# Stores of V, a reciprocal and the loads of new keys and values, moved between queues and steps of a transformer-layer kernel

## The chip, the cores and the metric

The kernel runs as one program on one core of a Trainium2 chip. The metric is the device time of that core in microseconds; the kernel before took 1255.03 us (median of three runs, 1254.48 to 1257.87).

A core has five engines with instruction queues of their own: TensorE (PE, matmuls), VectorE (DVE), ScalarE (ACT), GpSimd (POOL) and SyncE (SP), which only issues transfers here. They work on SBUF and PSUM and wait for each other by semaphores. A transfer is issued by an engine's queue (SPq, ACTq) and carried by 16 DMA engines.

## The reference

The layer is attention over paged keys and values, a long convolution of its output, and a feed-forward part with adapters, each added to its input. What the change touches is attention:

```python
q = rope(rmsnorm(x @ Wq.T)); k = rope(rmsnorm(x @ Wk.T)); v = x @ Wv.T
kc = k_cache[block_table].reshape(bsz, L, HK, D)     # 16 pages of 32 tokens
vc = v_cache[block_table].reshape(bsz, L, HK, D)
k_all = jnp.concatenate([kc, k], axis=1)             # 512 + 32 tokens
v_all = jnp.concatenate([vc, v], axis=1)
scores = jnp.einsum('bqhd,bkhd->bhqk', q, k_all) * SCALE
probs = jax.nn.softmax(jnp.where(valid, scores, -1e30), axis=-1)
o = jnp.einsum('bhqk,bkhd->bqhd', probs, v_all) @ Wo.T
```

There are 32 batches of 32 tokens, 32 query heads and 8 key/value heads (HK) of 128 (D), all in float32.

## The kernel before

The work is done in two halves of 16 batches (HB). A half projects V, K and Q of its 512 tokens, goes through attention batch by batch, and then through the output product, the convolution and the feed-forward part. Each engine has a program written out by hand; the order within an engine is the order of its code, and semaphores tie the engines together. Loops over batches go two batches at a time, one for each of two sets of key and value buffers (`par`).

**The new keys and values** of the half are stored to DRAM (`k_new`, `v_new`) and loaded again per batch in the layout that attention wants. V has two column halves of four tiles each. The first (`store_v(0, m)`) is computed at the start and stored by SyncE (L454 to L457). The second is computed last, when attention has already begun: ScalarE copies each tile out of PSUM (L707), waits for its own copy and issues the store (L712). The staging buffer has two places, so tiles 2 and 3 wait for the store of the tile two before.

**SyncE in attention** (`load_kv`) issues for each batch 16 key pages of 128 KB (L470), the batch's new keys (L475), then, when `v_free` allows it, its new values (L480) and 16 value pages (L485). Batch 0 and 1 are loaded piecemeal ahead of the loop; the new values of both wait for all stores of V (`vn_out`).

**A step of attention** is one key/value head `g` of one batch; four steps are a quad, since GU = 4 and the last head of a quad is computed without the split into high and low parts. For step s:

- ScalarE makes the high part of the keys for step s + 2 (L815) in three of four steps, takes the exponential of step s with its row sum (L856), and does in certain steps the copies of q (L807, L808), of the output (L841), the spread of the new probabilities (L834) and the mask (L820, L821).
- GpSimd makes the low part of the keys (L630) in three of four steps, and then scales the probabilities of step s - 2 by the reciprocal of their row sum (L616 for the new tokens, L618 for the 512 cached ones).
- TensorE computes the scores in six matmuls (L1084 to L1095; it waits for the low part of the keys ahead of L1090) or two (L1072, L1074), turns the scaled probabilities of step s - 3 (L1107) and multiplies those of step s - 4 with the values (L1139). Once per quad it adds the new values (L1149, `values_new`).
- VectorE adds the mask and takes the row minimum (L1636), copies the turned probabilities of step s - 3 out of PSUM (L1642), waits for the exponential of step s and takes the reciprocal of its row sum (L1649). In steps 1 and 5 of a batch it then makes the low part of q for the next quad (L1595, `lower_q`).

The probabilities go through a ring of four places, `prob0` and three in `ring`.

Of the kernel before, what the change touches and what calls it, by code (L numbers as in the profile page):

```python
# [13 lines left out]
ds = bass.ds  # L14
# [91 lines left out]
def build(nc, xT_d, w_d, amat_d, bmT_d, kpages_d, vpages_d, lA_d, lB_d, rows_d, vcT_d, bp_d, dls_d,  # L106
# [6 lines left out]
    with ExitStack() as ctx:  # L113
# [290 lines left out]
        def _(sp):  # L404
# [46 lines left out]
            load_w(0, 3)  # L451

            with sp.Fori(0, HALVES) as h:
                for k, m in enumerate((2, 3, 0, 1)):  # L454
                    sp.wait_ge(v_read, h * (2 * TILES) + k + 1)
                    sp.dma_start(vn_d[ds(h * HB + 4 * m, 4), :, 0:D].rearrange("b (t a) d -> (b t) a d", a=GU),
                                 v_stage(0, m).rearrange("p (a d) -> p a d", a=GU)).then_inc(vn_out[m % 2], 16)  # L457
                with sp.Fori(0, 2) as i:
                    for n in range(4, 8):
                        load_w(h, n, i)  # L460
# [28 lines left out]
                def load_kv(b, par):  # L489
                    pages = page_registers(b)  # L490
                    sp.wait_ge(k_free, h * HB + b - 1)
                    load_key_pages(par, pages, 0, NPP)
                    load_new_keys(b, par)
                    sp.wait_ge(v_free, h * (HB - 1) + b - 1)
                    load_new_values(b, par, v_in[par])
                    for j in range(NPP):
                        load_value_page(par, j, pages[j])

# [15 lines left out]
                for j in range(NPP):  # L514
                    if j % 4 == 0:

                        sp.wait_ge(turned, NQK * (h + 1) - 6 + 2 * (j // 4))
                        sp.sem_inc(sp_past, 1)
                    load_value_page(0, j, pages[j])
                sp.wait_ge(proj_ready, PROJ * (h + 1))  # L520
                sp.sem_inc(sp_past, 1)
                pages = page_registers(1)
                load_key_pages(1, pages, 8, NPP)
                load_new_keys(1, 1)
                for n in range(2):
                    sp.wait_ge(vn_out[n], 8 * KU * (h + 1))
                load_new_values(0, 0, first_vnew_in)
# [138 lines left out]
        def _(act):  # L666
# [18 lines left out]
            with act.Fori(0, HALVES) as h:  # L685
# [10 lines left out]
                def store_v(col, m):  # L696

                    unit = m if col == 0 else TILES + NQK + m
                    act.wait_ge(proj_ready, h * PROJ + unit + 1)
                    if col == 0:  # L700
                        pass
                    elif m < 2:

                        act.wait_ge(kn_out[m % 2], 8 * KU * (h + 1))
                    else:
                        act.wait_ge(vn_out[m % 2], h * (8 * KU) + 48)
                    nc.scalar.activation(v_stage(col, m), bank(m if col == 1 and m < 2 else 4 + m), ACT.Copy)\  # L707
                        .then_inc(v_read, 1)
                    if col == 0:
                        return  # L710
                    act.wait_ge(v_read, h * (2 * TILES) + TILES + m + 1)
                    act.dma_start(vn_d[ds(h * HB + 4 * m, 4), :, D:2 * D]  # L712
                                  .rearrange("b (t a) d -> (b t) a d", a=GU),
                                  v_stage(1, m).rearrange("p (a d) -> p a d", a=GU))\
                        .then_inc(vn_out[m % 2], 16)

                def squares(n, i=0):

# [118 lines left out]
                def keep_o(b, u):  # L837
# [3 lines left out]
                    nc.scalar.activation(qo[:, ds(b * (HQ * SEQ) + u * GU * D, GU * D)], bank(6 + u), ACT.Copy)\  # L841
                        .then_inc(ot_read, 1)

                def step(b, par, g, first, last=False):
                    s = h * STEPS + b * HK + g
                    if (g + 2) % GU < NS and not (last and g + 2 >= HK):
# [18 lines left out]
                        keep_o(b - 1, g // GU)  # L865
                    if g == 3 and not last:
                        mask_of(b + 1, 1 - par)

                act.wait_ge(turn_read, h * NQK + NQK - LAG)
                upper_q(0, 0)  # L870
# [469 lines left out]
        def _(dve):  # L1340
# [181 lines left out]
            with dve.Fori(0, HALVES) as h:  # L1522
# [100 lines left out]
                def step(b, par, g, first):  # L1623
                    s = h * STEPS + b * HK + g
                    if g < HK:
# [5 lines left out]
                        if first and g == 1:  # L1631
# [3 lines left out]
                        at = 1024 * (g % 2) + 512 - SPLIT * PSIZE  # L1635
                        V.tensor_tensor_reduce(prob(g % PRING)[:, 0:LK], PS[:, at:at + LK], mask[:, par, :],  # L1636
                                               rq[:, par, g:g + 1], 3.0e38, ALU.add, ALU.min, smin[:, g:g + 1]).then_inc(masked, 1)
                    if not (first and g < 3):
                        dve.wait_ge(pt_ready, s - 2)
                        if not (first and g < 5):  # L1640
                            dve.wait_ge(pv_done, s - 4)
                        V.tensor_copy(probT[:, (g - 3) % 2, :], bank(4)).then_inc(pt_main, 1)  # L1642
                    if first and g == 1:
                        dve.wait_ge(exp_done, s)
                        V.reciprocal(rinv[:, 0:1], rsum[:, 0:1]).then_inc(rinv_ready, 1)
                    if g < HK and not (first and g == 0):

                        dve.wait_ge(exp_done, s + 1)
                        V.reciprocal(rinv[:, g:g + 1], rsum[:, g:g + 1]).then_inc(rinv_ready, 1)  # L1649
                        if g % GU == 1:  # L1650
                            nb, u = (b, 1) if g == 1 else ((b + 1) % HB, 0)
                            dve.wait_ge(qhi_ready, h * (QUADS + 1) + b * UNITS + g // GU + 2)
                            dve.sem_inc(dve_past, 1)
                            lower_q(u, ds(nb * (HQ * SEQ) + u * GU * D, NS * D))

                for g in range(HK):
                    step(0, 0, g, True)
# [196 lines left out]
```

## Time and profile before

| | |
|---|---|
| time, median of three runs | 1255.03 us |
| time of the profiled execution | 1256.73 us |
| its span | 1254.8 us |
| TensorE busy | 1228.1 us (98%) |
| VectorE, ScalarE, GpSimd busy | 808.2, 788.1, 749.5 us |
| granted TensorE clock | full |
| read from and written to HBM | 203.33 and 10.49 MB, 170 GB/s over the span |
| attention, first half | about 160 to 476 us |
| attention, second half | about 785 to 1100 us |

Busy time is the sum of an engine's instructions. Ends of matmuls are modelled, so a busy TensorE is not TensorE at its peak. A time in a timeline is counted from the start of the span. Line numbers in the profile are those of the kernel before; behind the change lines have other numbers.

### The profile page before, as it was taken

How to read it: one execution, taken by the hardware profiler on the slowest of the kernel's cores; microseconds unless marked ns; L12 is line 12 of the kernel's file. 1: busy time of each engine (PE TensorE's matmuls, PEld its weight loads, DVE VectorE, ACT ScalarE, POOL GpSimd, SP SyncE). 2: the span in 40 equal slices, each digit the busy share in tenths (PEclk: the TensorE clock that was granted, in tenths of full speed). 3: DMA queues.
4: the chain of work that ended last, by engine and by line, in shares of the span. 5: the costliest groups of instructions: out<-in, count | busy, mean ns of one | idle time of the engine just before them, and what ended most of it. 6: DMA issues, size and time to landing. Idle time of an engine off the chain costs nothing.

```text
span 1254.8 us, 28770 instructions
## 1 busy us (share of the span) xinstructions
PE 1228.1 (98%) x7378; PEld 1031.9 (82%) x7378; DVE 808.2 (64%) x1736; ACT 788.1 (63%) x2259; POOL 749.5 (60%) x884
## 2 busy tenths in 40 slices
PE   7999999999999999999999999999999999999998
PEld 6788888899999997865777888888999999888756
DVE  6976666667666778951459667666766676655422
ACT  5666677778777774432346666777777777744320
POOL 4343467888888875433233443788888888844320
PEclk9999999999999999999999999999999999999999
DMA  6524288998999955306135252998899999534300
GB/s 206 194 92 149 95 232 220 230 232 233 236 236 237 229 159 177 142 8 194 68 105 184 84 172 91 243 220 227 224 234 240 231 238 239 121 116 153 89 30 34
DMA packets 147978, 214.82 MB, mean 171 GB/s; under 512 B 24949, under 2 KB 119479, under 8 KB 142136
## 3 DMA queue, kind: packets, MB, share of 16 engines
q1 hardware_dynamic: 134792, 206.96, 60.2%
q10 hardware_dynamic: 13104, 6.94, 1.9%
q8 instruction: 30, 0.49, 0.2%
q14 instruction: 52, 0.43, 0.1%
HBM read 203.33 MB, written 10.49 MB: 170 GB/s over the span
## 4 chain that ended last, share of the span: by engine, by line
PE 74%; SPq 15%; issue 5%; DVE 3%; ACT 1%; DMA 1%; ACTq 0%; DVEq 0%
PE PS L1139 12%; PE PS L1107 6%; SPq L485 6%; SPq L470 6%; PE PS L1206 5%; PE PS L1197 5%; PE PS L1001 5%; PE PS L1203 5%; PE PS L1005 5%; PE PS L999 5%; PE PS L1149 3%; PE PS L1248 2%; PE PS L985 2%; PE PS L1072 2%; PE PS L1237 1%
## 5 line engine op out<-in xcount | busy, mean ns | idle before, releaser
L630 POOL TENSOR_TENSOR kv_parts<-kv,k_hi 128x544 fp32r<-128x544 f32 x192 | 258.4, 1346 | 59.9 <-ACT k_hi L815 59.7
L1139 PE MATMUL PS<-probT,kv 128*128 128x128 f32 x2048 | 270.3, 275 | 0.0
L590 POOL TENSOR_TENSOR ring_parts<-ring,kv_parts 128x512 fp32r<-128x512 f32 x96 | 126.0, 1318 | 209.9 <-ACT kv_parts L693 181.6
L1139 PEld LDWEIGHTS PS<-probT,kv 128*128 128x128 f32 x2048 | 248.8, 192 | 0.0
L856 ACT ACTIVATE ring<-ring,smin 128x544 f32<-128x544 f32 x192 | 142.9, 744 | 86.9 <-DVE smin L1636 86.6
L1642 DVE COPY probT<-PS 128x512 f32<-128x512 f32 x256 | 175.5, 686 | 5.4 <-PE PS L1107 5.4
L1636 DVE CUSTOM_DVE_ANT_0 ring<-PS,mask,rq 128x544 f32<-128x544 f32 x192 | 149.7, 780 | 38.2 <-PE PS L1095 28.7
L652 POOL TENSOR_TENSOR ring_parts<-ring,kv_parts 128x512 fp32r<-128x512 f32 x64 | 85.0, 1332 | 95.1 <-ACT kv_parts L906 95.1
L815 ACT ACTIVATE k_hi<-kv 128x544 fp32r<-128x544 f32 x192 | 124.6, 650 | 15.5 <-DMA kv<-k_new 9.6
L618 POOL TENSOR_SCALAR ring<-ring,rinv 128x512 f32<-128x512 f32 x192 | 133.1, 693 | 0.0
L1676 DVE TENSOR_TENSOR qo_parts<-qo,kv_parts 128x512 fp32r<-128x512 f32 x64 | 85.3, 1339 | 54.1 <-ACT kv_parts L914 51.5
L1107 PE MATMUL PS<-consts,ring 128*128 128x128 f32 x768 | 115.8, 273 | 3.2 <-DVE probT L1642 2.4
L616 POOL TENSOR_SCALAR ring<-ring,rinv 128x32 f32<-128x32 f32 x192 | 79.6, 415 | 62.3 <-DVE rinv L1649 62.3
L1649 DVE RECIPROCAL rinv<-rsum 128x1 f32<-128x1 f32 x254 | 41.6, 164 | 114.7 <-ACT ring L856 95.6
L999 PE MATMUL PS<-kv_parts 128*128 128x512 f32 x352 | 102.3, 411 | 3.1 <-ACT kv_parts L693 1.5
L1206 PE MATMUL PS<-qo_parts,kv_parts 128*128 128x512 f32 x256 | 101.9, 398 | 0.0
L1197 PE MATMUL PS<-kv_parts 128*128 128x512 f32 x256 | 101.9, 398 | 0.0
L1203 PE MATMUL PS<-kv_parts,ring_parts 128*128 128x512 f32 x256 | 100.2, 392 | 0.0
L906 ACT ACTIVATE kv_parts<-ring 128x512 fp32r<-128x512 f32 x64 | 40.2, 631 | 94.5 <-PE PS L1197 94.4
L1107 PEld LDWEIGHTS PS<-consts,ring 128*128 128x128 f32 x768 | 89.8, 140 | 8.1 <-DVE probT L1642 3.3
L1001 PE MATMUL PS<-kv_parts 128*128 128x512 f32 x352 | 95.2, 392 | 0.0
L1005 PE MATMUL PS<-ring_parts,kv_parts 128*128 128x512 f32 x352 | 94.8, 391 | 0.0
(218 smaller groups left out, 2743.9 us busy)
## 6 DMA issues: line engine op xcount, KB each, us to landing
kv<-in_kpages SPq DMA_DIRECT2D x512, 128.0 KB, 2.5
kv<-in_vpages SPq DMA_DIRECT2D x512, 128.0 KB
ring<-in_w SPq DMA_DIRECT2D x44, 1024.0 KB, 5.0
k_new<-kv ACTq DMA_DIRECT2D x16, 256.0 KB, 2.3
kv<-k_new SPq DMA_DIRECT2D x32, 128.0 KB, 2.5
kv<-v_new SPq DMA_DIRECT2D x32, 128.0 KB
kv<-in_xT SPq DMA_DIRECT2D x8, 256.0 KB, 5.2
ring<-in_w SPq DMA_DIRECT2D x8, 256.0 KB, 5.4
```

The source lines that it names most:

```text
L630: nc.gpsimd.tensor_tensor(kbuf_lo(par)[:, :, g, :], kbuf(par)[:, :, g, :], k_hi[:, e % 2, :].rearrange("p (j t) -> p j t", t=PSIZE), ALU.s ...
L856: nc.scalar.activation(a, a, ACT.Exp, scale=-1.0, bias=smin[:, g:g + 1], accum_out=rsum[:, g:g + 1]).then_inc(exp_done, 1)
L999: nc.tensor.matmul(dst, x_hi[:, c, ms], hi[:, c, :], start=(c == 0), stop=False)
L1001: nc.tensor.matmul(dst, x_lo[:, c, ms], hi[:, c, :], start=False, stop=False)
L1005: mm = nc.tensor.matmul(dst, x_hi[:, c, ms], lo[:, c, :], start=False, stop=(c == KC - 1))
L1107: mm = nc.tensor.transpose(PS[:, 2048 + c * P:2048 + (c + 1) * P], prob(g % PRING)[:, c * P:(c + 1) * P], ident)
L1139: mm = nc.tensor.matmul(PS[:, at:at + D], vbuf(bpar)[:, c, gg * D:(gg + 1) * D], probT[:, g % 2, c * P:(c + 1) * P], start=(c == 0 and a = ...
L1197: mm = nc.tensor.matmul(bank(c), whi[:, a, cs], ohi[:, a, :], start=(head == 0), stop=False)
L1203: nc.tensor.matmul(bank(c), w[:, cs], ohi[:, a, :], start=False, stop=False)
L1206: mm = nc.tensor.matmul(bank(c), whi[:, a, cs], o, start=False, stop=(head == HQ - 1))
L1636: V.tensor_tensor_reduce(prob(g % PRING)[:, 0:LK], PS[:, at:at + LK], mask[:, par, :], rq[:, par, g:g + 1], 3.0e38, ALU.add, ALU.min, smin ...
L1642: V.tensor_copy(probT[:, (g - 3) % 2, :], bank(4)).then_inc(pt_main, 1)
```

## The change

It has three parts.

1. **V's last four tiles are stored by SyncE.** ScalarE only copies them to the staging buffer. SyncE stores tiles 0, 1 and 2 behind value pages 3, 7 and 11 of batch 0, and tile 3 behind the new keys of batch 1, ahead of its wait for all stores of V.
2. **The reciprocal of a row sum is taken one step later.** In step g VectorE takes the reciprocal for step g - 1, between the masked scores and the copy.
3. **From batch 2 on ScalarE issues the loads of new keys and new values** of the next batch, the keys in step 1 (behind the copy of the output), the values in step 6 (behind the spread). The waits for `k_free` and `v_free` stand ahead of them. SyncE keeps its own waits for the pages, and the new keys and values of batches 0 and 1.

```diff
@@ SyncE
-                for k, m in enumerate((2, 3, 0, 1)):
-                    sp.wait_ge(v_read, h * (2 * TILES) + k + 1)
-                    sp.dma_start(vn_d[ds(h * HB + 4 * m, 4), :, 0:D].rearrange("b (t a) d -> (b t) a d", a=GU),
-                                 v_stage(0, m).rearrange("p (a d) -> p a d", a=GU)).then_inc(vn_out[m % 2], 16)
+                def store_values(col, m, order):
+                    sp.wait_ge(v_read, h * (2 * TILES) + col * TILES + order + 1)
+                    sp.dma_start(vn_d[ds(h * HB + 4 * m, 4), :, col * D:(col + 1) * D]
+                                 .rearrange("b (t a) d -> (b t) a d", a=GU),
+                                 v_stage(col, m).rearrange("p (a d) -> p a d", a=GU)).then_inc(vn_out[m % 2], 16)
+
+                for order, m in enumerate((2, 3, 0, 1)):
+                    store_values(0, m, order)
@@ load_kv
                     load_key_pages(par, pages, 0, NPP)
-                    load_new_keys(b, par)
                     sp.wait_ge(v_free, h * (HB - 1) + b - 1)
-                    load_new_values(b, par, v_in[par])
@@ batches 0 and 1
                     load_value_page(0, j, pages[j])
+                    if j % 4 == 3 and j < NPP - 1:
+                        store_values(1, j // 4, j // 4)
+                        sp.sem_inc(sp_past, 1)
...
                 load_new_keys(1, 1)
+                store_values(1, 3, 3)
                 for n in range(2):
                     sp.wait_ge(vn_out[n], 8 * KU * (h + 1))
@@ ScalarE, store_v
-                    if col == 0:
-                        return
-                    act.wait_ge(v_read, h * (2 * TILES) + TILES + m + 1)
-                    act.dma_start(vn_d[ds(h * HB + 4 * m, 4), :, D:2 * D]
...
@@ ScalarE, attention
+                def load_new_keys(b, par):
+
+                    act.wait_ge(k_free, h * HB + b - 1)
+                    act.sem_inc(act_past, 1)
+                    act.dma_start(kbuf(par)[:, NPP, :, :].rearrange("p (u g) t -> p u (g t)", u=UNITS),
+                                  kn_d[ds(h * HB + b, 1), :, :, :].rearrange("a u p n -> p (a u) n"))\
+                        .then_inc(k_in[par], 16)
+
+                def load_new_values(b, par):
+
+                    act.wait_ge(v_free, h * (HB - 1) + b - 1)
+                    act.sem_inc(act_past, 1)
+                    act.dma_start(vnew(par),
+                                  vn_d[ds(h * HB + b, 1), :, :].rearrange("o (t a) n -> (o a) t n", a=GU))\
+                        .then_inc(v_in[par], 16)
...
+                    if g == 1 and not (first or last):
+                        load_new_keys(b + 1, 1 - par)
+                    if g == 6 and not (first or last):
+                        load_new_values(b + 1, 1 - par)
@@ VectorE, step
+                    if g <= HK and not (first and g == 0):
+
+                        k = (g - 1) % HK
+                        dve.wait_ge(exp_done, s)
+                        V.reciprocal(rinv[:, k:k + 1], rsum[:, k:k + 1]).then_inc(rinv_ready, 1)
                     if not (first and g < 3):
                         dve.wait_ge(pt_ready, s - 2)
...
-                    if first and g == 1:
-                        dve.wait_ge(exp_done, s)
-                        V.reciprocal(rinv[:, 0:1], rsum[:, 0:1]).then_inc(rinv_ready, 1)
-                    if g < HK and not (first and g == 0):
-
-                        dve.wait_ge(exp_done, s + 1)
-                        V.reciprocal(rinv[:, g:g + 1], rsum[:, g:g + 1]).then_inc(rinv_ready, 1)
```

VectorE in the loop over batches, step 1 and the start of step 2. The instruction with the output `ring,smin` is the masked scores; the kernel before:

```order
L1642 COPY probT<-PS 128x512
L1649 RECIPROCAL rinv<-rsum 128x1
L1652 ISA
L1595 ISA
L1595 TENSOR_TENSOR q_lo<-qo,q_hi 128x384
L1628 REGISTER_ALU
L1636 ISA ring,smin<-PS,mask,rq 128x544
```

and the kernel behind the change:

```order
L1661 RECIPROCAL rinv<-rsum 128x1
L1663 REGISTER_ALU
L1666 COPY probT<-PS 128x512
L1669 ISA
L1614 ISA
L1614 TENSOR_TENSOR q_lo<-qo,q_hi 128x384
L1647 REGISTER_ALU
L1655 ISA ring,smin<-PS,mask,rq 128x544
```

The reciprocal stood between the copy and the low part of q, and stands ahead of the copy now, where it is that of the step before.

SyncE ahead of the value pages of batch 1, before:

```order
L475 DMA kv<-k_new 128x2x128
L480 DMA kv<-v_new 128x1x256 x2
L485 ISA
L485 DMA kv<-in_vpages 32x1024
L485 ISA
```

and now:

```order
L479 DMA kv<-k_new 128x2x128
L455 REGISTER_ALU
L456 ISA
L456 DMA v_new<-kv 512x1x128
L484 DMA kv<-v_new 128x1x256 x2
L489 ISA
```

The store of V's last tile has come between the new keys and the new values of batches 0 and 1; the wait for all stores is ahead of the new values in both.

## Rows read from the trace of the kernel before

**Rows 1.** Busy time in a stretch of attention, with PEclk, DMA share, GB/s.

```profile
265.00:445.00 180.00, 180.00 (x1371) 163.41 (x1371) 125.88 (x321) 140.85 (x358) 153.04 (x208) 1.00 0.94 235
```

**Rows 2.** Line 1149 in three stretches: count, min/median/max ns, first and last start.

```profile
L1149 PE MATMUL PS<-kv x60: 592/594/595, 181.2 to 461.7; 128*128 128x512 f32 x60
L1149 PE MATMUL PS<-kv x46: 592/594/595, 250.6 to 461.7; 128*128 128x512 f32 x46
L1149 PE MATMUL PS<-kv x60: 592/594/595, 806.1 to 1086.2; 128*128 128x512 f32 x60
```

**Rows 3.** Timeline of SyncE's queue: start us, us from first to last, count.

```profile
155.16 10.51 SPq L485 DMA_DIRECT2D kv<-in_vpages  x16
...
173.49 8.83 SPq L485 DMA_DIRECT2D kv<-in_vpages  x16
183.95 9.68 SPq L470 DMA_DIRECT2D kv<-in_kpages  x16
193.84 0.39 SPq L475 DMA_DIRECT2D kv<-k_new  x1
...
320.38 8.12 SPq L470 DMA_DIRECT2D kv<-in_kpages  x16
...
329.25 0.63 SPq L480 DMA_DIRECT2D kv<-v_new  x1
329.99 7.33 SPq L485 DMA_DIRECT2D kv<-in_vpages  x16
339.40 8.24 SPq L470 DMA_DIRECT2D kv<-in_kpages  x16
```

**Rows 4.** Waits of ScalarE and TensorE: us in total, times, longest.

```profile
ACT k_hi L815 <- DMA kv<-k_new: 9.6, 9, 1.7
PE PS L1107 <- DVE probT L1642: 2.4, 7, 0.6
```

**Rows 5.** Timeline of steps 5 and 6 of a batch, start us, us.

```profile
328.76 0.28 PE L1095 MATMUL PS<-k_hi,q_lo 128*128 128x256 f32 x1
329.27 0.78 DVE L1636 CUSTOM_DVE_ANT_0 ring<-PS,mask,rq 128x544 f32<-128x544 f32 x1 [0.69 <-PE PS L1095]
...
330.85 0.28 PE L1095 MATMUL PS<-k_hi,q_lo 128*128 128x256 f32 x1
330.97 0.16 DVE L1649 RECIPROCAL rinv<-rsum 128x1 f32<-128x1 f32 x1 [0.30 <-ACT ring L856]
331.30 0.56 DVE L1595 TENSOR_TENSOR q_lo<-qo,q_hi 128x384 fp32r<-128x384 f32 x1 [0.16 <-issue]
331.34 0.68 POOL L616 TENSOR_SCALAR ring<-ring,rinv 128x32 f32<-128x32 f32 x1 [0.97 <-DVE rinv L1649]
331.77 0.78 DVE L1636 CUSTOM_DVE_ANT_0 ring<-PS,mask,rq 128x544 f32<-128x544 f32 x1
331.99 0.69 POOL L618 TENSOR_SCALAR ring<-ring,rinv 128x512 f32<-128x512 f32 x1
332.64 1.34 POOL L630 TENSOR_TENSOR kv_parts<-kv,k_hi 128x544 fp32r<-128x544 f32 x1
334.92 0.29 PE L1090 MATMUL PS<-kv_parts,q_hi 128*128 128x288 f32 x1
```

**Rows 6.** Timeline where VectorE, with two SBUF inputs, meets GpSimd: two places.

```profile
488.78 1.29 POOL L652 TENSOR_TENSOR ring_parts<-ring,kv_parts 128x512 fp32r<-128x512 f32 x1 [1.49 <-ACT kv_parts L906]
489.24 1.39 DVE L1676 TENSOR_TENSOR qo_parts<-qo,kv_parts 128x512 fp32r<-128x512 f32 x1
...
790.58 0.28 POOL L616 TENSOR_SCALAR ring<-prob,rinv 128x32 f32<-128x32 f32 x1
790.84 0.68 POOL L618 TENSOR_SCALAR prob<-prob,rinv 128x512 f32<-128x512 f32 x1
791.31 0.62 DVE L1595 TENSOR_TENSOR q_lo<-qo,q_hi 128x384 fp32r<-128x384 f32 x1
```

**Rows 7.** Stores issued by ScalarE (L712), from issue to landing.

```profile
DMA to landing us min/median/max: 3.2/3.9/5.4
```

More of the change, by code:

```diff
@@ L708, in store_v @@
                         .then_inc(v_read, 1)
-                    if col == 0:
-                        return
-                    act.wait_ge(v_read, h * (2 * TILES) + TILES + m + 1)
-                    act.dma_start(vn_d[ds(h * HB + 4 * m, 4), :, D:2 * D]
-                                  .rearrange("b (t a) d -> (b t) a d", a=GU),
-                                  v_stage(1, m).rearrange("p (a d) -> p a d", a=GU))\
-                        .then_inc(vn_out[m % 2], 16)
                 def squares(n, i=0):
@@ L1642, in step @@
                         V.tensor_copy(probT[:, (g - 3) % 2, :], bank(4)).then_inc(pt_main, 1)
-                    if first and g == 1:
-                        dve.wait_ge(exp_done, s)
-                        V.reciprocal(rinv[:, 0:1], rsum[:, 0:1]).then_inc(rinv_ready, 1)
-                    if g < HK and not (first and g == 0):
-                        dve.wait_ge(exp_done, s + 1)
-                        V.reciprocal(rinv[:, g:g + 1], rsum[:, g:g + 1]).then_inc(rinv_ready, 1)
[L1650 to L1654, printed above, removed]
+                    if g < HK and g % GU == 1:
+                        nb, u = (b, 1) if g == 1 else ((b + 1) % HB, 0)
+                        dve.wait_ge(qhi_ready, h * (QUADS + 1) + b * UNITS + g // GU + 2)
+                        dve.sem_inc(dve_past, 1)
+                        lower_q(u, ds(nb * (HQ * SEQ) + u * GU * D, NS * D))
                 for g in range(HK):
```

## The prediction

> **What bounds the kernel now.** I read the granted clock and the busy table first. In a stretch of settled attention TensorE is busy in all of 180 us at the full clock, while VectorE, ScalarE and GpSimd are busy 70, 78 and 85% and the DMA engines 94% [rows 1]. So work taken from another engine is worth time only where TensorE waits for it, and an edit can cost time by making TensorE wait. A busy row can also hide a wait, since the ends of matmuls are modelled. I therefore measured the pace. The matmul of line 1149 runs once in every four steps (a step is one KV head of one batch), in two records. From the first of a group at 250.6 to the last record at 461.7 there are 46 records, so 22 intervals; the last record begins 0.5 us behind its group's first, and (461.2 - 250.6) / 22 = 9.57 us for four steps. A half of the kernel has 64 records, so 32 such quads. From 181.2 on there are 29 intervals in 280.0 us, 2.5 us more than 29 x 9.57. In the second half 29 intervals take 1085.7 - 806.1 = 279.6 us, 2.1 us more [rows 2]. These 4.6 us are all that attention loses beyond its settled pace.
>
> The queue of SyncE comes next. Its issues stand almost back to back: a batch's 16 key pages 8.12 us, 16 value pages 7.33 us, and the next batch's key pages begin 19.02 us after the last batch's (320.38 to 339.40). That is nearly TensorE's 2 x 9.57 = 19.14 us. Early in attention the queue is late: the keys of batch 2 (counted from 0) take 9.68 us to issue and its new keys go out at 193.84, and the batch's cycle is 20 us [rows 3]. ScalarE waited 9.6 us in nine places for a transfer of new keys to land [rows 4]. So the 4.6 us are SyncE's being late.
>
> **The reciprocal, one step later.** Before, VectorE's step is: scores with the mask (L1636), copy (L1642), reciprocal of this step's row sum (L1649), for which it waits on ScalarE's exponential. Now it is scores, reciprocal of the step before, copy. VectorE loses a wait; GpSimd gets each reciprocal later. The place that matters is steps 1 and 5, where the copy is followed by the subtraction that makes q_lo. GpSimd scales the row of step 5 (L616, L618) and only then makes the low part of the keys for step 8 (L630), for which TensorE waits at L1090.
>
> As it was [rows 5]: reciprocal 330.97; GpSimd begins at 331.34, 0.37 us on; L618 at 331.99; L630 from 332.64 to 333.98; TensorE needs it at 334.92. The slack is 0.94 us.
>
> As it will be, in the same clock. The scores end as before, so step 5's L1636 stays at 329.27. Its reciprocal (of step 4) is at 329.27 + 0.78 = 330.05, GpSimd's L616 at 330.42, L618 at + 0.26 (790.58 to 790.84 [rows 6]) = 330.68, to 331.37 (0.69). VectorE's copy starts about 0.1 us behind the start of the reciprocal, at about 330.2, takes 0.69 us, and asks for q_lo at about 330.9: in the middle of that L618. What happens then is in [rows 6]. A VectorE operation with both inputs in SBUF that starts beside a running GpSimd one ends 0.41 us (384 columns: 790.84 + 0.68 = 791.52 against 791.31 + 0.62 = 791.93) or 0.56 us (512 columns: 490.07 against 490.63) after the GpSimd one ends. It stood still until GpSimd was through. So q_lo ends at 331.37 + 0.41 = 331.78, and step 6's L1636, which starts 0.09 us before that end (331.30 + 0.56 against 331.77), is at 331.69. Without the collision it would be at 331.36, TensorE's L1095 of 330.85 plus the 0.51 us that lie between 328.76 and 329.27. The reciprocal of step 5 follows at 332.47, GpSimd at 332.84, L630 at + 0.26 + 0.65 = 333.75, and TensorE gets its operand 1.34 + 0.05 us later (0.05 is my estimate of the handover), at 335.14. It wanted it at 334.92: 0.22 us of waiting. The pattern returns every quad and is not worked off, since VectorE follows TensorE. Quads that have a successor: 2 x 31 = 62, so 62 x 0.22 = +13.6 us. Without the collision the operand is there at 334.81, 0.11 us early, and this term is 0; with 0.15 us more of delay on the way it is 23 us.
>
> The Trainium skill (SBUF — State Buffer, "SBUF: two separate sides") says that VectorE and GpSimd share a pair of SBUF ports as an exclusive lock: whichever starts first keeps it for the whole instruction and the other fully blocks, for a VectorE operation with two SBUF inputs too. The two pairs of rows agree (0.41 and 0.56 us behind GpSimd's end). By that rule the term is +13.6 us; by a shared bandwidth it would be near 0.
>
> What the late wait gives: VectorE no longer stands before L1649. TensorE waited for VectorE's copy only 2.4 us in all [rows 4], so the gain is 0 to 2.4 us. I take -2, since the copy no longer stands behind an exponential.
>
> **V's last tiles stored by SyncE.** ScalarE loses four waits and issues per half in the first steps of attention. SyncE gains them, three among batch 0's value pages, one behind batch 1's new keys. Its issue is 0.63 us (the nearest row, 329.25) and about 0.1 us around it. The 16 value pages took 10.51 us where later ones take 7.33: if the transfers pace them, the three stores cost nothing; if not, 3 x 0.73 = 2.2 us. The fourth costs more: right behind it SyncE waits until every store has landed, and a store from ScalarE lands after 3.2 to 5.4 us, median 3.9 [rows 7]. Behind that wait stand both new-value loads, batch 1's 16 value pages (173.49) and all of batch 2's keys (183.95). They move by 0.7 + 3.9 = 4.6 us, plus 0 to 2.2, less up to 1.5 because value pages that took 8.83 can go at 7.33: 3 to 7 us, taken as 4.5. Batch 2's last keys were already what ScalarE waited for, but the new keys (0.39 us of issue and a gap) no longer come last, -0.5 us; and TensorE comes later by itself by about 4 quads x 0.22 = 1 us, and has up to 1 us of slack in the second half. I take 2.5 us a half, +5 (0 to +12). What ScalarE saves gives nothing then, since the next keys decide.
>
> **New keys and values issued by ScalarE.** SyncE loses per batch 0.39 + 0.63 us and the gaps around them: 329.99 - 328.50 (end of the key pages) becomes about 0.2, so 1.3 us of 19.0. From batch 3 on it catches up, and the old 4.6 us of lateness go: -4.6 (0 to -4.6). ScalarE gains two issues per batch, some 0.4 and 0.65 us plus waits that are long met. It is 78% busy, so 15 us of 19.1, and 16 after. Behind the issue in step 1 stands the k_hi for step 4, behind that in step 6 the k_hi for step 9; k_hi for the same place has GpSimd busy with scaling until L630 at 332.64 anyway, and its slack grows with the later reciprocal. I cost it 0; without that cover it would be 0.5 us in each of 28 batches, 14 us. The bytes stay the same.
>
> The Trainium skill (DMA: Bandwidth & Descriptors, "Issuing engines are not separate DMA queues") speaks against this part: transfers from several engines interleave on the same 16 DMA engines, and only the issuing time is saved. The DMA share of 0.94 [rows 1] agrees that there is little room; by that rule the gain is at most the 1.3 us a batch, of which TensorE had 4.6 us in all to give back.
>
> **Sum.** +13.6 - 2 + 5 - 4.6 + 0 = +12.0 us. The profiled execution took 1256.73 us around a span of 1254.8; it is 1.7 us above the median of 1255.03. So the changed kernel's profiled execution would be at 1268.7 us and its median at 1267 us.
>
> **Rivals.**
> 1. The collision does not happen or costs nothing (q_lo is asked for at another moment, or GpSimd gives way as L616 did when it met q_lo): term one is 0 by the 0.11 us that are left. For it: the margin is a tenth of a microsecond, and GpSimd's spans are rough. Against it: four rows agree, and L618 covers 0.7 us around the moment. -2 + 5 - 4.6 = -1.6, so 1253 us.
> 2. Faster: SyncE's issue and VectorE's wait are the real pace, and TensorE's 9.57 us hold waits that the records hide. SyncE's settled batch goes to 19.0 - 1.3 = 17.7 us; if TensorE follows a third of that way, 0.43 us in each of 28 batches, it is 12 us less, so with rival 1's terms some 1241 us. For it: SyncE's 19.02 against 19.14 us. Against it: the quads keep 9.57 us from 250 on whether ScalarE waits for keys or not.
> 3. ScalarE becomes late: its exponentials and k_hi slip by the two issues, 14 us more, 1281 us with the rest. Its 16 of 19 us speak against it.
> 4. The store's wait costs the full 7 us per half and TensorE has no slack: 4.5 us a half more, 1276 us with the collision, 1262 without it. It decides from the point where batch 2's keys land later than the step that reads them, which they already do.
>
> **Numbers.** The forecast with its neighbours in size has 0.5, rival 1 0.2, rival 2 0.13, rival 3 0.07, rival 4 0.1. What a measurement here can tell from no change is 0.3%, 3.8 us: 1251.3 to 1258.8. Rival 1 lies half in it (0.1) and mostly else below (0.08), rival 2 below (0.13), and 0.07 of the forecast's own chance, with a third of the wait per quad and the store's wait near 0, ends in it. The rest is above. That gives faster 0.21, same 0.17, slower 0.62. The range 1248 to 1278 leaves out most of rival 2 and of rival 3; the forecast's own is 1258 to 1276.
>
> **What would show it.** Quads of L1149 apart by about 9.8 us instead of 9.57; q_lo (L1614 now) taking 0.9 us or more instead of 0.56; TensorE waiting at L1090 for L630 in some 60 places; the first value pages of batch 1 about 4 us later and one longer wait of SyncE before them; no wait of ScalarE for new keys, and a settled SyncE that waits for k_free. I am wrong if q_lo stays at 0.56 us, if GpSimd's L630 for steps 4 and 8 ends before TensorE's second score matmul, or if quads get shorter than 9.5 us.

## The result and the profile after

The changed kernel takes 1261.53 us (median of 18 executions, 1258.04 to 1267.01) against 1257.02 us of the kernel before (18 executions on the same chip): ratio 1.0037, 95% interval 1.0026 to 1.0047. It is slower, by 4.5 us where +12 was forecast. The profiled execution has a span of 1258.5 us, 3.7 us more than before's.

I read the pace of attention first. Line 1149 is line 1168 now; count, min/median/max ns, first and last start, in the stretches of [rows 2]:

```profile
L1168 PE MATMUL PS<-kv x60: 592/595/1215, 182.7 to 464.7; 128*128 128x512 f32 x60
L1168 PE MATMUL PS<-kv x48: 592/594/595, 245.3 to 464.7; 128*128 128x512 f32 x48
L1168 PE MATMUL PS<-kv x60: 592/595/1061, 809.0 to 1089.9; 128*128 128x512 f32 x60
```

From 245.3 on there are 23 intervals in 218.9 us (464.2 - 245.3): 9.52 us a quad, against 9.57 in [rows 2]. The settled pace is better, and not 9.8 us. But the first record comes 1.5 us later than before, and 29 intervals from it take 281.5 us against 280.0: all of the settled gain and more is lost before 245. The second half has 280.4 us against 279.6. And a maximum of 1215 ns stands where [rows 2] has 595. The stretch of [rows 1] shows the settled part again: the same 235 GB/s, the full clock, and VectorE busy 7 us less for one instruction more.

```profile
265.00:445.00 180.00, 179.76 (x1385) 166.68 (x1384) 118.96 (x322) 142.36 (x362) 152.14 (x208) 1.00 1.00 235
```

The low part of q is line 1614 now. Min/median/max ns:

```profile
L1614 DVE TENSOR_TENSOR q_lo<-qo,q_hi x66: 546/550/577, 159.2 to 1092.8; 128x384 fp32r<-128x384 f32 x66
```

Not one of the 66 takes 0.9 us: q_lo is not held anywhere. Here is the same place of a quad as in [rows 5], in step 1 of a batch and the step behind it (there it was steps 5 and 6), in the changed kernel (timeline; start us, us; L1655 are the scores, L1661 the reciprocal, L1666 the copy, L622 and L624 GpSimd's scaling, L636 the low part of the keys, L1109 TensorE's use of it):

```profile
342.33 0.78 DVE L1655 CUSTOM_DVE_ANT_0 ring<-PS,mask,rq 128x544 f32<-128x544 f32 x1 [1.43 <-PE PS L1114]
343.04 0.16 DVE L1661 RECIPROCAL rinv<-rsum 128x1 f32<-128x1 f32 x1
343.11 0.67 DVE L1666 COPY probT<-PS 128x512 f32<-128x512 f32 x1
343.55 0.29 POOL L622 TENSOR_SCALAR ring<-prob,rinv 128x32 f32<-128x32 f32 x1 [0.68 <-DVE rinv L1661]
343.70 0.55 DVE L1614 TENSOR_TENSOR q_lo<-qo,q_hi 128x384 fp32r<-128x384 f32 x1
343.81 0.99 POOL L624 TENSOR_SCALAR prob<-prob,rinv 128x512 f32<-128x512 f32 x1
...
345.12 0.16 DVE L1661 RECIPROCAL rinv<-rsum 128x1 f32<-128x1 f32 x1
...
345.48 0.29 POOL L622 TENSOR_SCALAR ring<-ring,rinv 128x32 f32<-128x32 f32 x1 [0.68 <-DVE rinv L1661]
...
346.40 1.34 POOL L636 TENSOR_TENSOR kv_parts<-kv,k_hi 128x544 fp32r<-128x544 f32 x1
...
347.97 0.30 PE L1109 MATMUL PS<-kv_parts,q_hi 128*128 128x288 f32 x1
```

q_lo begins 0.11 us ahead of L624 and goes first; it is L624 that is longer, 0.99 us instead of 0.69. In the 23 quads from 245 to 465 q_lo begins between 0.12 us ahead of L624 and 0.02 us behind it, and goes first every time. L636 ends at 347.74, 0.23 us before the matmul of L1109 starts, and 0.11 us before the load of its weights (347.85).

So the loss is elsewhere. The waits of TensorE on transfers (us in total, times, longest); the kernel before has no such wait:

```profile
PE PS L1158 <- DMA kv<-in_vpages: 4.7, 2, 2.8
PE PS L1168 <- DMA kv<-v_new: 2.5, 1, 2.5
```

And SyncE's queue, against [rows 3] (L456 is the store, L484 the new values, L489 value pages, L474 key pages):

```profile
172.78 0.39 SPq L479 DMA_DIRECT2D kv<-k_new  x1
173.43 0.59 SPq L456 DMA_DIRECT2D v_new<-kv  x1
177.88 1.49 SPq L484 DMA_DIRECT2D kv<-v_new  x2
179.58 7.58 SPq L489 DMA_DIRECT2D kv<-in_vpages  x16
```

Between the end of the store's issue (174.02) and the new values SyncE stands for 3.9 us, as forecast, and batch 1's value pages go out at 179.58 instead of 173.49. Of these 6.1 us the wait is 3.9, the store's own issue 0.6, and 1.6 were lost before, at the first three stores (the new keys go out at 172.78 instead of 171.20). What the forecast did not see is who waits. TensorE, around the two waits of the first half:

```profile
182.73 2.07 PE L1168 MATMUL PS<-kv 128*128 128x512 f32 x2 [2.45 <-DMA kv<-v_new]
183.81 1.23 PE L1103 MATMUL PS<-k_hi,q_hi 128*128 128x288 f32 x1
...
187.23 0.38 PE L1103 MATMUL PS<-k_hi,q_hi 128*128 128x288 f32 x1
...
195.00 1.16 PE L1158 MATMUL PS<-probT,kv 128*128 128x128 f32 x8 [1.87 <-DMA kv<-in_vpages]
```

The pair L1168, 1.02 us elsewhere, takes 2.07 here. The windows show why (busy time of PE, PEld, DVE, ACT, POOL, then the granted clock, the DMA share and GB/s):

```profile
176.00:182.00 6.00, 4.28 (x33) 3.78 (x32) 2.91 (x8) 5.57 (x15) 5.61 (x8) 1.00 0.26 72
182.00:188.00 6.00, 5.27 (x26) 4.24 (x27) 1.63 (x5) 0.80 (x2) 1.18 (x3) 0.72 1.05 210
188.00:194.00 6.00, 5.12 (x41) 4.68 (x40) 4.30 (x13) 5.80 (x16) 5.21 (x7) 1.00 1.08 206
194.00:200.00 6.00, 5.00 (x24) 4.08 (x25) 1.13 (x4) 1.19 (x4) 2.38 (x4) 0.72 0.97 301
```

Behind each of the two idle times the clock stood at its lower level, 1.2 GHz, for about 3.4 us (0.28 x 6 / 0.5), and came back to 2.4 GHz. The step from 182.73 to 187.23 takes 4.50 us; the same step at the full clock, 349.81 to 352.68 below, takes 2.87. So in this execution a wait of 2.45 us cost 4.1 us. In the second half the new values come in time, and TensorE waits 2.84 us for value pages (at 820.63), again with the lower clock behind it.

```profile
349.81 1.02 PE L1168 MATMUL PS<-kv 128*128 128x512 f32 x2
350.27 0.69 PE L1103 MATMUL PS<-k_hi,q_hi 128*128 128x288 f32 x1
...
352.68 0.38 PE L1103 MATMUL PS<-k_hi,q_hi 128*128 128x288 f32 x1
```

### The profile page after: what moved, and what is told of

It reads as the page before. It is cut to its first block, busy times and chain, and to the rows that moved or that the text cites. A ratio compares the mean times of both kernels' runs of the same rounds, so it can differ in the third digit from the quotient of the medians.

```text
span 1258.5 us, 28890 instructions
## 1 busy us (share of the span) xinstructions
PE 1227.6 (98%) x7378; PEld 1041.6 (83%) x7378; DVE 782.7 (62%) x1736; ACT 790.1 (63%) x2259; POOL 746.2 (59%) x884
## 4 chain that ended last, share of the span: by engine, by line
PE 85%; SPq 5%; issue 3%; DMA 3%; DVE 2%; ACT 1%; ACTq 0%; POOL 0%; DVEq 0%; POOLq 0%
PE PS L1158 16%; PE PS L1126 8%; PE PS L1225 5%; PE PS L1216 5%; PE PS L1020 5%; PE PS L1024 5%; PE PS L1222 5%; PE PS L1018 5%; PE PS L1168 4%; SPq L489 3%; PE PS L1267 2%; PE PS L1091 2%; PE PS L1093 2%; PE PS L1004 2%; PE PS L1109 2%
## 5 line engine op out<-in xcount | busy, mean ns | idle before, releaser
L636 POOL TENSOR_TENSOR kv_parts<-kv,k_hi 128x544 fp32r<-128x544 f32 x192 | 257.8, 1343 | 22.4 <-ACT k_hi L814 22.4
L1655 DVE CUSTOM_DVE_ANT_0 ring<-PS,mask,rq 128x544 f32<-128x544 f32 x192 | 150.2, 782 | 173.6 <-PE PS L1114 112.5
L1666 DVE COPY probT<-PS 128x512 f32<-128x512 f32 x256 | 172.1, 672 | 5.5 <-PE PS L1126 5.5
L624 POOL TENSOR_SCALAR ring<-ring,rinv 128x512 f32<-128x512 f32 x192 | 133.2, 694 | 0.0
L1572 DVE TENSOR_TENSOR kv<-PS,kv 128x512 f32<-128x512 f32 x80 | 55.2, 689 | 61.1 <-ACT prob L729 31.4
L1103 PE MATMUL PS<-k_hi,q_hi 128*128 128x288 f32 x192 | 93.0, 485 | 0.0
```

The lines of the kernel that those rows point to most:

```text
L636: nc.gpsimd.tensor_tensor(kbuf_lo(par)[:, :, g, :], kbuf(par)[:, :, g, :], k_hi[:, e % 2, :].rearrange("p (j t) -> p j t", t=PSIZE), ALU.s ...
```

## The experiments

Theory A: the reciprocal and ScalarE's loads are gains, the stores on SyncE are a loss larger than both, and the collision is real but was missed by a tenth of a microsecond. Theory B: the change behaves as forecast, with the terms a little smaller. e1 to e4 ran on one chip, e5 to e8 on one, e9 to e12 on one; every ratio is to executions of the kernel before on the same chip.

**e1: parts two and three, the stores left with ScalarE.** Against the changed kernel:

```diff
@@ SyncE
-                    if j % 4 == 3 and j < NPP - 1:
-                        store_values(1, j // 4, j // 4)
...
-                store_values(1, 3, 3)
@@ ScalarE, store_v
...
+                    act.wait_ge(v_read, h * (2 * TILES) + TILES + m + 1)
+                    act.dma_start(vn_d[ds(h * HB + 4 * m, 4), :, D:2 * D]
...
```

> The stores of V stay on ScalarE; the later reciprocal and the loads by ScalarE are in. Theory A (the fourth store and the wait for all stores behind it, on SyncE, cost the start of attention; the other two parts are a gain): the waits of TensorE for new values (2.5 us) and for value pages (4.7 us) are gone, the old 4.6 us of lateness too, and the settled quad stays at 9.50 us: 6 to 9 us below before, 1248 to 1251 where before is 1257. Theory B (ScalarE's two issues per batch or the later reciprocal cost the time, and the stores are harmless): as slow as the changed kernel, +3 to +5 us. Theory C (ScalarE needs to be free of the stores for the loads to pay): -2 to +1 us.

1250.75 us, ratio 0.9948 [0.9934, 0.9963]. Two of the three parts make the kernel faster by 6.5 us, and in their trace TensorE waits for no transfer of values.

**e2: the reciprocal alone.** Only VectorE's `step` is as in the changed kernel.

```diff
+                    if g <= HK and not (first and g == 0):
+                        k = (g - 1) % HK
+                        dve.wait_ge(exp_done, s)
+                        V.reciprocal(rinv[:, k:k + 1], rsum[:, k:k + 1]).then_inc(rinv_ready, 1)
```

> Only the reciprocal is one step later. By the prediction's collision it would cost 62 x 0.22 = 13.6 us. By theory A it costs nothing; the question is whether it gives the settled gain of 0.07 us per quad: if VectorE's wait for the exponential was what stretched one quad in four to 9.71 us, the quads go to 9.50 and the time falls by 2 to 4 us; if the lateness of new keys stretched them, they stay at 9.57 and the time is the same within 1 us.

1254.09 us, 0.9974 [0.9964, 0.9984]: 3.3 us faster. In the first half of its trace quads settle (from 309 on) at 9.48 to 9.54 us, on average 9.50 instead of 9.57; in the second half five of the later ones still take 9.6 to 10.0. ScalarE's wait for new keys has grown from the 9.6 us of [rows 4]:

```profile
ACT k_hi L815 <- DMA kv<-k_new: 14.7, 16, 2.4
```

A faster TensorE runs into SyncE's lateness here.

**e3: ScalarE's loads alone.** Only `load_kv` and ScalarE's two new functions are as in the changed kernel.

```diff
@@ SyncE, load_kv
-                    load_new_keys(b, par)
...
-                    load_new_values(b, par, v_in[par])
@@ ScalarE, attention
+                    if g == 1 and not (first or last):
+                        load_new_keys(b + 1, 1 - par)
+                    if g == 6 and not (first or last):
+                        load_new_values(b + 1, 1 - par)
```

> Only the loads of new keys and values go to ScalarE. Theory A: the 4.6 us of lateness early in attention go, and if new keys were what stretched the settled quads, they go to 9.50 and 8 us are gained; if VectorE's wait did, they stay at 9.57 or get longer, since exponentials come later by the issue ahead of them and VectorE stands behind them: -4 to 0 us. Theory B: +3 us or more.

1253.27 us, 0.9973 [0.9963, 0.9983]: 3.4 us faster. Settled quads keep 9.57 us, and the lateness ahead of them is gone: over all 64 records of the first half (first to last start) the kernel before takes 294.8 us and this one 292.1. In the second half it is 293.8 and 291.6 us (by the first record of the last group). Attention is 4.9 us shorter in this trace, then, where the forecast had 4.6; the time gains less, and in this trace two stretches at the lower clock (at about 171 and 795 us), which the kernel before does not have, stand ahead of these records. The two gains have different places, and they add: 3.3 + 3.4 = 6.7 against the 6.5 of e1.

```profile
L1167 PE MATMUL PS<-kv x64: 592/594/596, 182.5 to 474.6; 128*128 128x512 f32 x64
```

**e4: the stores alone.**

```diff
+                    if j % 4 == 3 and j < NPP - 1:
+                        store_values(1, j // 4, j // 4)
...
+                store_values(1, 3, 3)
@@ ScalarE, store_v
...
-                    act.wait_ge(v_read, h * (2 * TILES) + TILES + m + 1)
-                    act.dma_start(vn_d[ds(h * HB + 4 * m, 4), :, D:2 * D]
...
```

> Only V's last four tiles are stored by SyncE. Theory A: TensorE waits for new values and value pages at the start as in the changed kernel, and SyncE, which keeps all loads, does not catch up: +8 to +14 us, quads at 9.57. Theory B: 0 to +1 us.

1267.52 us, 1.0078 [1.0064, 1.0091]: 9.8 us slower. TensorE waits at the same two lines as in the changed kernel:

```profile
PE PS L1140 <- DMA kv<-in_vpages: 6.4, 3, 3.5
PE PS L1150 <- DMA kv<-v_new: 2.1, 2, 1.9
```

- 3.3 - 3.4 + 9.8 = +3.1 us, against 4.6 [3.3, 5.9] of the whole (1.0037): the parts explain the change, to 1.5 us.

**e5: the wait for all stores behind the value pages.** The changed kernel, but SyncE waits ahead of batch 0's new values only for the stores with which they come, and for the last one only ahead of batch 1's.

```diff
+                sp.wait_ge(vn_out[0], h * (8 * KU) + 48)
+                load_new_values(0, 0, first_vnew_in)
+                for j in range(NPP):
+                    load_value_page(1, j, pages[j])
                 for n in range(2):
                     sp.wait_ge(vn_out[n], 8 * KU * (h + 1))
-                load_new_values(0, 0, first_vnew_in)
                 load_new_values(1, 1, v_in[1])
-                for j in range(NPP):
-                    load_value_page(1, j, pages[j])
```

> The whole change, but SyncE waits only for the stores of V's tile 0 before it loads batch 0's new values, then issues batch 1's 16 value pages, and only then waits for all stores and loads batch 1's new values. Theory A (the wait for all stores is the cost): the 4 to 5 us of waiting per half are hidden behind 7.6 us of issues, TensorE's waits for new values and pages go, and the time falls from +4.6 to -3 to -7 us against before. Theory B (three more issues among batch 0's value pages are the cost): it stays at +2 to +5 us.

1254.29 us, 0.9985 [0.9977, 0.9994]. Where the wait for all stores stands is worth 6.5 us of the changed kernel (1.0037 - 0.9985 = 0.0052). SyncE no longer stands still ahead of the value pages, and TensorE's wait for them is 0.2 us. Its wait for new values has not gone, as Theory A had it: 1.9 us in two places. And ScalarE waits 18.6 us in 14 places for key pages, against 2.8 in the changed kernel. SyncE's queue:

```profile
173.37 0.59 SPq L456 DMA_DIRECT2D v_new<-kv  x1
174.14 1.00 SPq L484 DMA_DIRECT2D kv<-v_new  x1
175.37 8.76 SPq L489 DMA_DIRECT2D kv<-in_vpages  x16
184.30 0.63 SPq L484 DMA_DIRECT2D kv<-v_new  x1
```

**e6: the fourth store back on ScalarE.** The other three stay on SyncE.

```diff
@@ SyncE
-                store_values(1, 3, 3)
@@ ScalarE, store_v
+                    if col == 1 and m == 3:
+                        act.wait_ge(v_read, h * (2 * TILES) + TILES + m + 1)
+                        act.dma_start(vn_d[ds(h * HB + 4 * m, 4), :, D:2 * D]
...
```

> The whole change, but V's very last tile is stored by ScalarE as before, which issues it about 6 us earlier than SyncE does in its queue. Theory A: the wait for all stores is nearly over when SyncE comes to it; time -4 to -7 us against before, what is left above parts 2 and 3 alone being the three stores. Theory B: the three stores among the value pages put SyncE 2 us late, so +0 to +3 us.

1253.97 us, 0.9980 [0.9968, 0.9991]: 7.2 us better than the changed kernel, the same as e5. The three stores among the value pages keep the rest, 0.9980 against 0.9948 of e1, so 4 us. They show in when batch 2's keys begin; e6 first, then e1:

```profile
186.38 9.36 SPq L474 DMA_DIRECT2D kv<-in_kpages  x16
```

```profile
182.94 8.51 SPq L470 DMA_DIRECT2D kv<-in_kpages  x16
```

**e7: a pause ahead of q_lo.** e1 with a reciprocal of 32 columns on VectorE between the copy and the low part of q, to bring the collision about.

```diff
                         dve.sem_inc(dve_past, 1)
+                        V.reciprocal(small[:, 1, :], con("iota")[:, 1:33])
                         lower_q(u, ds(nb * (HQ * SEQ) + u * GU * D, NS * D))
```

> Parts 2 and 3 of the change, with one more small VectorE instruction (a reciprocal of 32 constants, about 0.3 us, to scratch) between the copy and q_lo in steps 1 and 5. If GpSimd's row scaling holds VectorE when it starts first (the prediction's collision, which missed by a few tenths of a microsecond), q_lo takes 0.9 to 1.1 us instead of 0.55, the next masked scores start 0.4 us later and TensorE waits 0.1 to 0.2 us in each of 62 quads: 6 to 12 us slower than parts 2 and 3 alone, so 0 to +6 us against before. If there is no such hold, q_lo stays at 0.55 us and the time within 1 us of parts 2 and 3 alone, -6 us.

1255.74 us, 1.0000 [0.9988, 1.0012]. Here the collision is, and not in every quad. Two neighbours, from two timelines (L1670 is the pause, L616 GpSimd's 512 columns, L1613 q_lo):

```profile
349.24 0.34 DVE L1670 RECIPROCAL small<-consts 128x32 f32<-128x32 f32 x1
349.31 0.70 POOL L616 TENSOR_SCALAR prob<-prob,rinv 128x512 f32<-128x512 f32 x1
349.50 0.91 DVE L1613 TENSOR_TENSOR q_lo<-qo,q_hi 128x384 fp32r<-128x384 f32 x1
...
359.04 0.34 DVE L1670 RECIPROCAL small<-consts 128x32 f32<-128x32 f32 x1
359.13 1.13 POOL L616 TENSOR_SCALAR prob<-prob,rinv 128x512 f32<-128x512 f32 x1
359.30 0.49 DVE L1613 TENSOR_TENSOR q_lo<-qo,q_hi 128x384 fp32r<-128x384 f32 x1
```

In the first q_lo begins 0.19 us behind GpSimd and ends 0.40 us after it (350.41 against 350.01; [rows 6] had given 0.41). In the second it begins 0.17 us behind and goes first all the same, and GpSimd's instruction is held. Quads alternate between 9.49 and 9.70 to 9.81 us. The two rows stand for all: in the 62 quads in which the two instructions meet, q_lo goes first in all 30 where it begins at most 0.17 us behind GpSimd, and is held in all 32 where it begins 0.18 to 0.27 us behind.

**e8: the same pause behind q_lo.** The control: the same work, and no collision.

```diff
                         lower_q(u, ds(nb * (HQ * SEQ) + u * GU * D, NS * D))
+                        V.reciprocal(small[:, 1, :], con("iota")[:, 1:33])
```

> The same as the last, but the small instruction stands behind q_lo, where it can meet nothing. It is the control: q_lo at 0.55 us, quads at 9.50 us, -6 us against before, whatever theory holds. If it is as slow as the last, the last shows only VectorE's added 0.3 us and no collision.

1248.88 us, 0.9939 [0.9926, 0.9952]. Two kernels with the same instructions, in another order at one place, are 6.9 us apart: half of the forecast's term of 13.6, with q_lo held in half of the quads.

**e9: a longer pause.** 48 columns in place of 32.

```diff
-                        V.reciprocal(small[:, 1, :], con("iota")[:, 1:33])
+                        V.reciprocal(small[:, 0:2, 0:24], con("iota")[:, 1:49].rearrange("p (a b) -> p a b", a=2))
```

> Parts two and three alone, with a reciprocal of 48 columns (e7's had 32) on VectorE ahead of each q_lo in attention. In e7 q_lo was 0.19 us behind the start of GpSimd's 512-column scaling in every second quad and stood behind it (0.91 us), and 0.17 us behind it in the others and went first (0.49 us); quads alternated between 9.49 and 9.72 to 9.78. 16 columns more are about 0.1 us more of delay. Theory (the order of two starts decides, the margin was 0.02 us): now every q_lo is blocked, every quad is about 9.75, so 62 x 0.25 = 15 us more than the same pause behind q_lo, ratio to the kernel before about 1.006. Rival (a delayed quad leaves room to the next whatever the pause is): quads go on alternating, 7 us more, ratio 1.000.

1263.03 us, 1.0064 [1.0051, 1.0078]. Now q_lo is held in 60 of the 62 quads in which it meets GpSimd, in all but one of each half; it begins 0.24 to 0.38 us behind GpSimd there:

```profile
L1613 DVE TENSOR_TENSOR q_lo<-qo,q_hi x66: 494/809/854, 159.7 to 1095.8; 128x384 fp32r<-128x384 f32 x66
```

```profile
345.31 0.19 PEld L1108 LDWEIGHTS PS<-kv_parts,q_hi 128*128 128x128 f32 x1 [0.23 <-POOL kv_parts L628]
```

The prediction had said 0.22 us of waiting at this instruction, in some 60 places. The view of waits counts 60, 16.0 us in all:

```profile
PEld PS L1108 <- POOL kv_parts L628: 16.0, 60, 1.4
```

A quad takes (464.5 - 249.4) / 22 = 9.78 us:

```profile
L1167 PE MATMUL PS<-kv x46: 592/594/596, 249.4 to 465.0; 128*128 128x512 f32 x46
```

**e10: the longer pause behind q_lo.** e9 with the two lines exchanged.

```diff
                         lower_q(u, ds(nb * (HQ * SEQ) + u * GU * D, NS * D))
+                        V.reciprocal(small[:, 0:2, 0:24], con("iota")[:, 1:49].rearrange("p (a b) -> p a b", a=2))
```

> Control of e9: the same 48-column reciprocal, behind q_lo. Both theories: q_lo stays at 0.55 us, quads at 9.50, ratio about 0.994, as e8's 0.9939. If the work of the pause costs VectorE time by itself, it is this one that is slower.

1248.89 us, 0.9947 [0.9933, 0.9961]; quads of (467.6 - 249.5) / 23 = 9.48 us. e9 is 14.1 us slower, where the prediction's term was 13.6. The two agree better than they should: a settled quad of e9 is 0.29 us longer, not 0.22, which is 18 us in 62 quads, but early in each half e10 has one slow quad (11.23 and 9.98 us) that e9 has not, so the slower pace hides some lateness of the transfers.

```profile
L1167 PE MATMUL PS<-kv x48: 592/594/596, 249.5 to 468.1; 128*128 128x512 f32 x48
```

**e11: the changed kernel with the pause of e9.** The same one line ahead of `lower_q`, in the changed kernel: the collision and the stores together.

> The changed kernel with the 48-column reciprocal ahead of each q_lo. It is the case of the forecast, with the collision that did not come by itself. Theory (collision and the stores' late loads add up): 1261.5 + 15 = 1276 us, ratio about 1.015; quads 9.75. Rival (TensorE's slower quads hide SyncE's late loads, or the other way about): 5 to 8 us less than that, ratio 1.009 to 1.011.

1273.58 us, 1.0140 [1.0124, 1.0155], 13 us above the changed kernel's 1.0037. Without the stores the collision cost 14.1 us (e9 against e10), so the terms add, to within the intervals; the rival expectation, that one hides the other, falls.

**e12: e1 again.**

> e1 again, so that e9 to e11 have the kernel without a pause on the same chip. Ratio 0.995 as in e1, if the pause behind q_lo is free the same as e10 within 0.2%. If e1's gain was of its chip, nearer to 1.

1248.52 us, 0.9942 [0.9928, 0.9956]. It confirms e1, and equals e10: the pause behind q_lo costs nothing. What ScalarE still waits for in its trace are key pages, 12.3 us in ten places, so SyncE's queue is not early even without the new keys and values. Of all versions this one (with e8 and e10, which only add to it) is the fastest: it beats the kernel before by 0.5 to 0.6% and the changed one by 0.9%.

## Why the prediction was wrong

The direction was right and the size was not. That the direction was right is luck: without the collision the forecast's own sum is -1.6 us, and what made the kernel slower is the stores, twice what I took. Two errors, +13.6 and -4.8, stood in the sum and partly cancelled.

- **The collision (+13.6, measured 0). This is the step that failed**, in "as it will be, in the same clock". The mechanism was right, and nearly its price: e9, where it was brought about, shows 0.23 us of waiting in the row above, 0.27 us on average in 60 places, and 14.1 us in all. What was wrong were the two moments, and so the order of the two instructions. In the clock of [rows 5], with L1636 at 329.27, I had q_lo at 330.9 and L618 at 330.68. The changed kernel has q_lo 1.37 us behind the start of the scores (343.70 - 342.33), so at 330.64, and L624 at + 1.48, so at 330.75. I had q_lo 0.22 us behind, and it is 0.11 us ahead. Both hang on the start of the reciprocal, so that this starts 0.71 us behind the scores and not 0.78 moves them together and decides nothing. Of the 0.33 us between, 0.19 are VectorE's: the copy starts 0.07 us behind the reciprocal (I had 0.15), and q_lo starts 0.08 us before the copy ends, where I let it start at its end. The other 0.14 are GpSimd's: it begins 0.51 us behind the start of the reciprocal (343.04 to 343.55), where I took the 0.37 us of [rows 5]. More rows of the same pair would not have mended that. From 245 to 465 us the trace of the changed kernel has 45 handovers to an idle GpSimd that take 0.35 to 0.37 us, the one at 345.12 among them, and only those of steps 1 and 5 take longer: 23 of them, of 0.39 to 0.52, in a pattern that returns every four quads (about 0.50, 0.39, 0.51, 0.47), as the code of the loop over two batches does. There GpSimd scales the first head of a quad, and in the program it then waits for a second semaphore (`new_turned`) before it starts; in [rows 5] it scaled the second head, and did not. That fits, but no run takes the second wait out. The margin was smaller than what my rows could carry, and I gave the collision half of the chance. Rival 1 said just this (0.2); with its other terms it came to -1.6 us.
- **The stores (+5, measured 9.8 alone).** The event was as forecast: SyncE stands 3.9 us, everything behind it moves, and the three stores cost 1.6 us of the queue's time (0 to 2.2 forecast) and 4 us of the kernel's (e6 against e1). I read its price off batch 2's keys, since ScalarE's wait for keys was the one that [rows 4] showed. But new values of batch 0 stand behind the same wait, and TensorE needs them at 180.3; they and batch 1's value pages made TensorE wait 2.45 and 1.87 us in the first half. And in this trace each of these waits was followed by some 3.4 us at the lower clock, 1.6 us more for the first; the sum had no term for the clock. The term was mis-sized then: 9.8 and not 5. Rival 4 without the collision gave 1262 us, and 1261.5 was measured, but that is chance: from the 1255.0 us it started from it is +7.4, and measured are +4.5 from 1257.0. Its event, 4.5 us a half more than I took, is borne out by half (2.4 a half more).
- **VectorE's lost wait (-2, measured -3.3).** The bound of 2.4 us came from a row that names the copy as releaser; the load of the weights of L1107 also came late without a named releaser, by 15.8 us in 62 places, and in e2 by 2.1 us in 8. How much of that was TensorE's time the view does not say; the shorter quads of e2 do (0.07 us each).
- **ScalarE's loads (-4.6, measured -3.4).** Right in place (the early lateness, nothing of the settled pace) and nearly in size. ScalarE's wait for new keys fell from 9.6 us in nine places to 2.0 us in one in the changed kernel. Rival 3 falls: settled quads are no longer. Rival 2's mechanism falls with e3, where SyncE has less to issue and settled quads keep 9.57 us.

By the sum with the measured terms: 0 - 3.3 + 9.8 - 3.4 = +3.1; measured +4.5. The 1.4 us between stay unexplained. They are within the intervals of e2 to e4, and the profiled changed kernel has four stretches at the lower clock where that of e4 has two, so it may be an effect of both parts together; no run separates these.

## What to carry to other kernels

A term that hangs on which of two instructions starts first is a coin until the moments are better known than their distance. Take every handover from rows of the same step of the program, with the same waits ahead of the instruction: rows of the same two engines in other steps were all alike here (0.35 to 0.37 us), and all too short. If two moments stay closer than about 0.3 us, price both outcomes and let neither be the centre. When a wait is put into a queue, list every transfer behind it with the moment at which its reader needs it, not only the one whose reader waits already; the first one due decides. Test the parts of a change one by one: here two gains of some 3 us each were hidden under one loss of 10.

## What the runs showed of the hardware

- **Who goes first at SBUF.** VectorE with two SBUF inputs and GpSimd exclude each other in either direction, and GpSimd's scaling is held as well: 0.69 us becomes 0.99 to 1.13. The recorded start does not quite decide: q_lo went first in all 30 quads of e7 where it was recorded at most 0.17 us behind GpSimd, and was held in all 32 where it was 0.18 us or more behind, as it was in 60 quads of e9, 0.24 to 0.38 us behind. So VectorE seems to have a start of some 0.18 us on the record. That is one pair of instructions, and it may be otherwise for others. A held q_lo ends 0.40 us behind GpSimd's instruction; a held scaling ends some 0.5 us behind q_lo. The Trainium skill (SBUF — State Buffer, "SBUF: two separate sides") gives the exclusive lock and the first to start; the runs agree, with this offset beside it.
- **The clock behind a wait.** TensorE's granted clock fell to 1.2 GHz for about 3.4 us behind idle times of 2.45 and 1.87 us in the first half of the changed kernel, and behind 1.84 us (for the low part of the keys, at 796.88) and 2.84 us in the second. The length of the idle time alone does not decide it. The changed kernel has the same wait of 1.84 us at 169.05, with the full clock behind it. And e4 has its two waits of the first half, of 1.93 and 2.72 us, without a fall; the second, and the window around it:

```profile
194.68 0.49 PE L1140 MATMUL PS<-probT,kv 128*128 128x128 f32 x2 [2.72 <-DMA kv<-in_vpages]
```

```profile
194.00:200.00 6.00, 5.32 (x40) 4.84 (x41) 1.96 (x5) 1.75 (x5) 1.90 (x4) 1.00 0.82 243
```

  Nor does the program decide it. e1 and e12 are the same kernel, and TensorE waits 1.14 and 1.16 us in them shortly before 170.3. Behind it the clock falls in e1 and not in e12; e1 first:

```profile
170.00:176.00 6.00, 5.80 (x36) 5.80 (x37) 2.70 (x9) 3.63 (x10) 4.77 (x8) 0.72 0.75 215
```

```profile
170.00:176.00 6.00, 6.00 (x50) 5.80 (x51) 4.04 (x10) 4.36 (x12) 5.57 (x8) 1.00 0.74 205
```

  The executions of the changed kernel, 1258 to 1267 us, spread more than those of the kernel before (1254.35 to 1259.33), and their mean clocks lie between 0.993 and 0.999. What decides in which of them the clock falls stays open.
